# Attention with a gated FFN: the projection block rebuilt, with three and a half FFN chunks beside it instead of two

## What is computed

```
xn  = layernorm(X)
Q, K, V = xn @ Wq.T, xn @ Wk.T, xn @ Wv.T          # 16 heads of 16, rotary positions on Q and K
s   = softmax(causal(Q K.T / 4)) V  @ Wo.T
h   = fwht(xn * SU_ug) / 64                        # Walsh-Hadamard over 256 features
y   = silu(h @ W_gate.T * (..)) * (h @ W_up.T * (..))     # 1024 features
y   = fwht(y * SU_dp) / 64 @ W_down.T * (..)
out = X + s * silu(y)
```

## Time and profile before

| | |
|---|---|
| median of 3 runs | 883.9 us (883.43 to 888.3) |
| the profiled execution | 882.72 us, its span 881.0 us |
| granted TensorE clock, mean | 0.972 |
| TensorE busy | 798.3 us |
| VectorE, ScalarE, GpSimd busy | 574.3, 498.6, 421.1 us |
| block two begins on TensorE | 218.85 us |

### The profile page before, as it was taken

The page is one execution under the profiler, slowest core; times in us unless marked ns, Lnnn a source line. Parts: engine busy times, 40 slices in busy tenths (PEclk is TensorE's granted clock), DMA queues, the critical chain, the costliest instruction groups (busy, mean ns, idle before and its releaser), DMA issues.

```text
span 881.0 us, 14276 instructions
## 1 busy us (share of the span) xinstructions
PE 798.3 (91%) x5136; PEld 482.1 (55%) x5136; DVE 574.3 (65%) x1016; ACT 498.6 (57%) x687; POOL 421.1 (48%) x472
## 2 busy tenths in 40 slices
PE   3767899887989999999999999999999999999976
PEld 2545777766655555555555555555555555555523
DVE  3997455324776777667777677766767666776444
ACT  3434453532455667566775666764676657666560
POOL 3776573563641455225671544543384424745311
PEclk9999999999999999999999999999999999999987
DMA  8445233525502322233344342334433232532131
GB/s 277 155 149 175 69 119 124 174 79 201 124 1 73 89 57 61 86 96 88 94 118 153 111 116 85 85 103 124 125 116 98 89 108 61 167 93 94 57 128 48
DMA packets 61294, 96.21 MB, mean 109 GB/s; under 512 B 10344, under 2 KB 27432, under 8 KB 61224
## 3 DMA queue, kind: packets, MB, share of 16 engines
q1 hardware_dynamic: 59640, 93.47, 34.8%
q10 hardware_dynamic: 1584, 1.84, 0.6%
HBM read 58.06 MB, written 36.95 MB: 108 GB/s over the span
## 4 chain that ended last, share of the span: by engine, by line
PE 60%; DVE 8%; ACT 4%; issue 2%; POOL 1%; ACTq 0%; DVEq 0%; POOLq 0%
PE ps L295 15%; PE ps L1291 13%; PE ps L1275 10%; PE ps L1252 8%; PE ps L305 8%; DVE ps L1526 3%; PE ps L1327 3%; ACT probs L1421 2%; DVE mx L1531 2%; PE ps L1263 2%; ACT x_ffn L1433 1%; DVE ps L1588 1%; DVE y_sb L342 1%; ACT y_sb L330 1%; ACT a_sb L315 0%
## 5 line engine op out<-in xcount | busy, mean ns | idle before, releaser
L1421 ACT ACTIVATE probs<-ps 128x1024 f32<-128x1024 f32 (+1 forms) x320 | 291.7, 940 | 103.6 <-PE ps L1275 102.5
L1531 DVE TENSOR_REDUCE mx<-ps 128x4 f32<-128x512 f32 (+1 forms) x192 | 216.0, 1134 | 110.9 <-PE ps L1252 63.3
L1147 POOL TENSOR_SCALAR_AFFINE_SELECT probs<-probs 128x256 f32<-128x256 f32 (+1 forms) x192 | 92.5, 486 | 271.6 <-ACT probs L1421 271.0
L1526 DVE CUSTOM_DVE_ANT_0 ps<-ps,tri 128x384 f32<-128x384 f32 (+1 forms) x256 | 154.4, 647 | 39.0 <-PE ps L1252 39.0
L1291 PE MATMUL ps<-probs,v_ones 128*32 128x512 f32 (+3 forms) x1536 | 157.7, 498 | 5.5 <-POOL probs L1147 5.0
L1275 PE MATMUL ps<-q_s,k_s 64*128 64x512 f32 (+3 forms) x768 | 147.6, 410 | 8.4 <-ACT probs L1421 4.3
L1275 PEld LDWEIGHTS ps<-q_s,k_s 64*128 64x128 f32 x768 | 67.3, 184 | 151.9 <-issue 79.5
L1252 PE MATMUL ps<-k_s,q_s 48*128 48x512 f32 (+3 forms) x768 | 123.0, 369 | 8.4 <-PEq L386 5.2
L295 PE MATMUL ps<-xh,wug_hi 128*128 128x512 f32 x256 | 110.5, 432 | 16.8 <-DVE a_sb L336 16.4
L350 POOL TENSOR_TENSOR a_sb<-a_sb,u_sb 128x512 f32<-128x512 f32 x64 | 82.2, 1287 | 62.7 <-DVE a_sb L336 34.4
L295 PE MATMUL ps<-xh,wug_lo 128*128 128x512 f32 x256 | 102.8, 402 | 0.0
(11 more groups left out here) (134 smaller groups left out, 1073.9 us busy)
## 6 DMA issues: line engine op xcount, KB each, us to landing
scr_qk<-kinds SPq DMA_DIRECT2D x64, 256.0 KB, 2.3
q_s<-scr_qk SPq DMA_DIRECT2D x64, 128.0 KB, 2.8
...
```

The costliest lines, as they stand in the source:

```text
L1147: pool.affine_select(out=part, in_=part, compare_op=ALU.is_ge, fill=0.0, base=0, pattern=pattern, channel_multiplier=-1).then_inc(cut, 1)
L1421: act.activation(probs[:, n % 2, p, :, 0:w], ps[:, bank:bank + 2, 0:w], ACT.Exp, scale=SCALE).then_inc(exp_ok, 1)
L1526: last = dve.tensor_tensor_reduce(part_of, part_of, sh.tri[:, CH - w:CH], 1.0, LOWEST, ALU.add, ALU.max, mx[:, v % 2, kind, h, i % TPC:i % ...
L1531: last = dve.tensor_reduce(out[:, :, pairs[0]:pairs[0] + n], ps[:, banks[0]:banks[0] + 2, 0:n * w].rearrange('p e (x k) -> p e x k', x=n), ...
```

## The change

Block one:

- `fold_up` is gone. TensorE makes sum and difference by accumulation: four float32 matmuls for a part instead of two, with `had` and a negated copy `minus_had`. All four parts have buffers and are loaded at the start, in the order UG_PARTS. FOLDS puts parts 0 and 1 before k = 0, 2 and 3 into k = 0, and the two of the down weights into k = 1.
- The shift moves from VectorE (`centre`) to GpSimd (inside `rsqrt`), from a small VectorE copy `minus_mean`. The last stage of `fold_down` moves from GpSimd to VectorE, and so does the low part of Q for k = 1 and 2.
- FFN jobs start at k = 1, place 2: chunks 0, 1 and 2 and the first 8 gate and up jobs of chunk 3 run in block one, 80 jobs instead of 48. Gates and ups stand four to a place in places 2 and 3 of odd k and 0 and 1 of the next; downs stand in places 0 and 1 of odd k from 3.
- All 8 PSUM banks are given out by age over the written sequence (`early_banks`), for the projections, the folds and the FFN alike.
- `kinds_low(7, 1)` and `kinds_high(7, 1)` come before the last jobs; gates of an FFN chunk are stored when it is done; FFN_ORDER says which tokens FFN chunk n holds.

Block two: it starts with 112 FFN jobs instead of 144; chunk 3's rest and chunks 4 to 7. The constants are set in z = 0, x for the first 'turn' is loaded first, its normalising is spread over z = 1 to 3, and the split of Wo moves from z = 3 to z = 4. At the end, `divide(6)` moves from round z = 83 to 82, the spreading of the last unit's inverse into round 84, and the high and low parts of chunk 6 behind the rounds.

```diff
-for n, counts in ((0, ((3, (3, 3, 3, 3)), (4, (2, 2, 2, 2)), (5, (2, 2, 0, 0)))),
-                  (1, ((5, (0, 0, 3, 3)), (6, (5, 5, 2, 2)), (7, (1, 1, 1, 1))))):
...
+FFN_ORDER = (4, 0, 1, 2, 3, 5, 6, 7)
...
+NEARLY = 3
...
+for n in range(NEARLY + 1):
     todo = gates_and_ups(n) + downs(n)
-    for k, numbers in counts:
+    for k, numbers in ((2 * n + 1, (0, 0, 4, 4)), (2 * n + 2, (4, 4, 0, 0)), (2 * n + 3, (4, 4))):
+        if k >= NCHUNK:
+            break
...
+UG_PARTS = (2, 0, 3, 1)
+FOLDS = {(-1, 0): (0, 1), (0, 0): (2,), (0, 2): (3,), (1, 1): (4,), (1, 2): (5,)}
+        width = 1 if turn != what or what[0] in ('gate', 'up') else 2
+        sets = [tuple(range(b, b + width)) for b in range(0, 8, width)]
+        banks = min(sets, key=lambda bs: max(held[b][1] for b in bs))
...
-for n in range(2, NCHUNK):
-    todo += gates_and_ups(n)
...
+for n in range(NEARLY, NCHUNK):
+    todo += [j for j in left_over if j[0] != 'down'] if n == NEARLY else gates_and_ups(n)
+    turns = [('turn', n + 1, d) for d in range(DC)] if n + 1 < NCHUNK else []
...
-jobs_at[round_of(NU - 1, 0) + 3].append(('divide', LAST - 1, 0))
+jobs_at[round_of(NU - 1, 0) + 2].append(('divide', LAST - 1, 0))
...
                 pool.tensor_tensor(sh.rstd[:, ORDER[c], :], var_eps[:, :], minus_half[:, :], op=ALU.pow).then_inc(rstd_ok, 1)
+                pool.wait_ge(rstd_ok, c + 1)
+                pool.tensor_tensor(sh.shift_x[:, ORDER[c], :], minus_mean[:, c % 2, :], sh.rstd[:, ORDER[c], :],
+                                   op=ALU.mult).then_inc(centred, 1)
...
+            fold_down(0)
             rsqrt(1)
...
+                    pe.wait_ge(ug_in[i], 16)
+                    for o in range(DC):
+                        pe.matmul(ps[:, bank + o, :], had[:, :], wug[:, i, 0, :], start=True, stop=False)
+                        last = pe.matmul(ps[:, bank + o, :], (minus_had if o else had)[:, :], wug[:, i, 1, :], start=False,
+                                         stop=True)
...
+                if c >= 3 and c % 2:
+                    act.wait_ge(sh.gate_ok, IB * (c - 1) // 2)
+                    act.wait_ge(sh.up_ok, IB * (c - 1) // 2)
...
-            def fold_up(i):
-                dve.wait_ge(ug_in[i % 2], 16 * (i // 2 + 1))
...
+            def fold_down_last():
+                dve.wait_ge(d_fold, 2)
...
+                if z == 0:
+                    constants()
...
             end_high(LAST - 1)
+            high_part(LAST - 1)
             take_heads(NU - 1, 1)
```

More of the change, by code:

```diff
@@ L125 @@
     chain_at[round_of(NU - 1, 0) + later, what] = LAST - 1
-for what, later in (('load', 2), ('recip', 3), ('keep', 4)):
+for what, later in (('load', 2), ('recip', 3), ('keep', 3), ('spread', 4)):
     chain_at[round_of(NU - 1, 0) + later, what] = LAST
@@ L552, in _ @@
                         rsqrt(k + 2)
-                    if place == 2 and k < 3:
+                    if place == 2 and k < 1:
                         queries_low(k)
@@ L593, in features @@
                 bank = pair_at[turn]
[L594 removed]
+                wait_banks(turn)
                 par = c % 2
@@ L651, in fold_weights @@
                 else:
                     pe.wait_ge(d_fold, 3)
-                for o in range(2):
-                    k = 4 * (i - NUG) + 2 * o
-                    rhs = fold[:, i % 2, o, :] if i < NUG else wd[:, 1, k:k + 2, :]
-                    last = pe.matmul(ps[:, bank + o, :], had[:, :], rhs, start=True, stop=True)
+                    for o in range(2):
+                        k = 4 * (i - NUG) + 2 * o
+                        last = pe.matmul(ps[:, bank + o, :], had[:, :], wd[:, 1, k:k + 2, :], start=True, stop=True)
@@ L657, in fold_weights, with folds @@
                 last.then_inc(prod, 1)
+            def folds(k, place):
+                for i in folds_at(k, place):
+                    fold_weights(i)
             pe.wait_ge(ident_ok, 1)
             transposes(0)
+            folds(-1, 0)
             for k in range(NCHUNK):
@@ L667, in _ @@
                     job(j)
+                folds(k, 0)
                 features(k, 1)
@@ L670, in _ @@
                     job(j)
+                folds(k, 1)
                 if k + 1 < NCHUNK:
@@ L674, in _ @@
                     job(j)
+                folds(k, 2)
                 pe.wait_ge(wq_ok, 2)
@@ L678, in _ @@
                     job(j)
-                for i in (2 * k, 2 * k + 1):
-                    if i < NW:
-                        fold_weights(i)
+                folds(k, 3)
         @block.scalar
@@ L860, in jobs @@
                         outer_gate(dve, ps, sh, early_bank[turn_of(j)], *j[1:3])
+                for i in folds_at(k, place):
+                    weights_low(i)
             variances(0)
-            centre(0)
-            weights_rest(0)
-            take_xl(0)
-            variances(1)
-            weights_rest(1)
-            dve.wait_ge(small_in, 32)
+            dve.wait_ge(had_in, 16)
+            dve.tensor_scalar_mul(minus_had[:, :], had[:, :], -1.0).then_inc(had_ok, 1)
+            dve.wait_ge(scales_in, 16)
             dve.tensor_scalar_mul(su_ug_s[:, :], su_ug[:, :], float(D) ** (-0.5)).then_inc(scale_ok, 1)
@@ L974, in second_block @@
         block = ctx.enter_context(nc.Block())
-        pair_round = lambda n, ib: max(job_round['gate', n, ib], job_round['up', n, ib])
+        pair_round = lambda n, ib: max(job_round.get((kind, n, ib), -1) for kind in ('gate', 'up'))
         ups = lambda z: [j for j in jobs_at[z] if j[0] in ('gate', 'up') and z == pair_round(*j[1:])
-                         and (j[0] == 'up' or ('up', *j[1:]) not in jobs_at[z])] if z >= 0 else []
+                         and (j[0] == 'up' or ('up', *j[1:]) not in jobs_at[z])] if z >= 0 else [
+                             j for j in jobs_in(LAST, PLACES - 1) if j[0] == 'up']
         nth_x = lambda n: n - NEARLY - 1
@@ L1487, in _ @@
                     take_heads(u - 1, 1)
-                if at(z, 'high') is not None:
+                if at(z, 'high') is not None and at(z, 'high') < LAST - 1:
                     high_part(at(z, 'high'))
-                if 0 <= z - 1 < NR:
+                if z < NR:
+                    normalise_at(z)
+                if z < NR:
                     for j in ups(z - 1):
@@ L1629, in _ @@
                     invert(at(z, 'recip'))
-                if z >= round_of(NU - 1, 0):
-                    if at(z, 'scale') is not None:
-                        scale_heads(at(z, 'scale'))
-                    if at(z, 'low') is not None:
-                        low_part(at(z, 'low'))
+                if z >= round_of(NU - 1, 0) and at(z, 'scale') is not None:
+                    scale_heads(at(z, 'scale'))
             end_low(LAST - 1)
+            low_part(LAST - 1)
             scale_heads(LAST)
```

301 lines of the change are left out of this document (149 added, 152 removed).

## The result

The changed kernel takes 848.1 us (median of 4 runs, 846.2 to 848.5) where the kernel before, on the same chip, takes 883.7: a ratio of 0.9575 with a 95% interval of 0.9544 to 0.9606, so 4.25% less (by the two medians alone 35.5 us, 4.0%). The profiled execution took 848.0 us with a span of 846.2, 34.8 less than the span before.

A forecast was written before the change was run, and what follows sets the result against it. TensorE was taken to bound attention (z = 6 to 79), while block one had idle time. From 881.0, +9.7 - 2.9 - 29 - 5.6 gave 853.2, with 1.7 around the span 854.9; forecast 856 us, range 842 to 871.

The forecast's parts named there:

- the main case: Whole kernel: both stages, block one and the rounds, go as worked out, 849 to 864 us; chance 0.66.
- z = 0 to 5: Block two's first rounds: matmuls +1.4, wait before the first turn -3.0, less time at 1.2 GHz -1.3; sum -2.9 us.
- Waits in block one: Block one: 8 us of TensorE waits in all, 5 worked out and 3 for the unseen; last job at 225.
- The chain of even k: Block one, k = 2, 4, 6: K, `turn`, `rotate`, `hidden_low`, tanh, up and x's split delay the next X about 1 us each.
- The edge: From block one's last job to block two: 3.5 us, taken between 2.5 and 5.2; block two begins at 228.5, +9.7.
- nothing, or 2 us: z = 1: price if GpSimd's constants, issued in z = 0, delay `hidden` and so the tanh of pair 7.
- The rounds: z = 6 to 79: 31 jobs fewer, 0.82 us saved per job going from two to one, 1.5 from three; -29 us.
- The rival of rounds that don't shrink: z = 6 to 79: thinner rounds run one after another, -18 instead of -29, total 867 us; chance 0.12.
- the one that they shrink whole: z = 6 to 79: TensorE's time comes back whole, -43 instead of -29, total 842 us; chance 0.08.
- The end: Last rounds: fewer jobs in z = 80 -2.3, chunk 6's split behind the last exponentials -3.3; sum -5.6 us.
- The rival on the other side: Block one: its chain holds TensorE, slower than before; block one grows by 36 more, total 891 us; chance 0.07.
- VectorE and GpSimd hinder each other: Block one: some 19 VectorE instructions with both inputs in SBUF take 1.1 us longer; 15 on the path, 870; chance 0.07.

The follow-up runs named there:

- the second profile: The changed kernel run once more, unedited, as the base for two other runs on their chip: 845.9 us, ratio 0.9576 to the kernel before.

## Why the prediction was right, point by point

The forecast was 856, and the median is 848.1: inside the stated 842 to 871, but 1 us under the 849 to 864 of the main case, to which 0.66 was given. 854.9 was predicted for the profiled execution, which took 848.0. Changes of each stage, from the earlier trace rows:

| | predicted | measured |
|---|---|---|
| block two begins | +9.7 | +1.6 (+3.9 in the second profile) |
| z = 0 to 5 | -2.9 | +1.2 (-0.3) |
| z = 6 to 79 | -29 | -32.2 (-33.4) |
| the end | -5.6 | -5.5 (-7.2) |
| span | -27.8 | -34.8 (-36.9) |

The four stages miss by 8.1 us too high, 4.1 too low, 3.2 too high and 0.1 too low. That the sum is only 7 off is in part luck, since the 4.1 stand against the others.

- **Work in block one: right.** The sum of jobs, projections and folds was 194.2; TensorE is busy 194.35. Q(0) began at 21.6 (22.9 taken): the folds at the lower clock cost less than the 2 us.
- **Waits in block one: right in kind and place, too large in size.** The term of 8 us (5 worked out, 3 for what I didn't see) measured 3.4: 0.83 three times and 0.9 once, none over 2. The chain of even k was named, at about 1 us each time, and is the one that shows; the 0.9 stands in k = 1 and is a wait for VectorE's `turn`, where 1 to 2 us were taken for VectorE (its cause is in the last point of this list). The further 3 us for the unseen had nothing behind them.
- **The edge: at the wrong end of its bounds.** I took 3.5 between 2.5 and 5.2, and it is 1.04, under the lower one. The bound counted a tanh, an up and a barrier; the tanh runs under TensorE's last products, and the up's 0.69 and 0.3 of barrier are left. With 48 and with 72 jobs, where nothing stands behind the projections, it is 7.0: the cover by the last eight jobs was the right reason.
- **z = 0 to 5: the step that failed.** The wait of 2.99 before the first turn is gone, as said, and the 1.4 us of matmuls came. But new waits took the gain: in z = 1 TensorE waits 1.71 for a gate's sum on VectorE, after the turn 0.95 and 0.69, in z = 5 0.82, 0.55 and 0.29, and six matmuls after these run at the lower clock. That is 5.0 us of waits where the kernel before had 3.5. In its timeline:

```profile
231.27 2.55 POOL L375 TENSOR_TENSOR a_sb<-a_sb,u_sb 128x512 f32<-128x512 f32 x2
232.60 0.62 ACT L1477 CAST hid_hi<-a_sb 128x512 fp32r<-128x512 f32 x1 [2.33 <-POOL a_sb L375]
...
235.84 0.50 PE L320 MATMUL ps<-xh,wug_hi 128*128 128x512 f32 x1 [1.71 <-DVE a_sb L361]
```

  I had left this open with "nothing, or 2 us", because GpSimd's constants stand ahead of `hidden` in z = 1. It is of that size. The trace leads back to the constants: GpSimd works on block one's last two pairs till 225.5 and on the constants till 231.3, then comes `hidden`, behind it `hidden_high` on ScalarE, the tanh at 234.38, the gate's sum at 235.09 and the product. With 48 and with 72 jobs no pairs are left over at the edge, GpSimd sets the same constants before the first `hidden` is due, and TensorE has no such wait. That the wait goes when the constants do was not shown (the run with them in z = 1 has no profile to read). The second profile of the changed kernel has the same six waits to 0.01 us, but a clock of 1.00 instead of 0.97 and 49.6 us for this stage: 1.5 of the 4 us missed are the clock.
- **The rounds: right, with a term each way.** -32.2 against -29 (place by place 30). The one-job rounds take 6.66, 6.54, 6.99, 6.38 and 6.35 by place in the unit (medians), 32.9 in all against the 33.3 of the earlier trace rows; the two-job rounds 37.8, so that a job is worth 0.98 and not 0.82. With 48 jobs the stage was already 552.0, 4.8 less at one job less, a part that the sum didn't have: four rounds with 'turn' jobs (z = 16, 31, 45, 61) went from 8.34, 8.03, 8.11 and 8.34 to 7.34, 7.13, 6.89 and 7.36, 4.1 in all. The other 30 jobs take off 27.4, 0.91 each, and 1.04 without the 3.8 that the empty round took back. The rival of rounds that don't shrink (867) is out, and so is the one that they shrink whole, at 1.39. The other way, a round with no job was put at 0.5 us under a one-job round: z = 51 with 52 cost 17.2 instead of 13.45 with one job each, and a job put back there gains 1.1 to 3.8, as the clock goes.
- **The end: right.** -5.5 against -5.6, with the mechanism named: the last weighting waits 4.15 us where the split is left in its round and 2.69 where it isn't, and leaving it costs 2 to 4 us. Late next is GpSimd's cut; `low_part`, which the prediction named, holds the first piece by 0.92 in the second profile alone.
- **The rival on the other side** (block one's chain holds TensorE, 891) needed 28 us more of waits and had none. The order of its risk was right all the same: one more pass of GpSimd in seven chunks costs 6.7 us from Q(0) on, and two banks 23.
- **VectorE and GpSimd hinder each other** (870): they do, but not at that price. The mean of VectorE's row with both inputs in SBUF (L848) is 1468 ns, shorter than before (1572), with ten more pairs of GpSimd beside it, and GpSimd's own two are 4% longer (1385 and 1338 against 1330 and 1289). Single instructions show what the means hide. One line's durations, then one long instruction of that line, and two that start together:

```profile
L848 DVE TENSOR_TENSOR kinds<-rot,kinds x15: 1217/1226/2286, 42.9 to 215.6; 128x1024 fp32r<-128x1024 f32 x15
```

```profile
42.86 2.25 DVE L848 TENSOR_TENSOR kinds<-rot,kinds 128x1024 fp32r<-128x1024 f32 x1
...
107.31 1.22 DVE L848 TENSOR_TENSOR kinds<-rot,kinds 128x1024 fp32r<-128x1024 f32 x1
107.32 1.26 POOL L520 TENSOR_TENSOR shift_x<-minus_mean,rstd 128x4 f32<-128x4 f32 x1
```

  The shift takes GpSimd 0.20 to 0.52 us six times, and 1.26 and 1.27 the two times that it starts with such an instruction of VectorE: it ends with that one. At 59.44, during a pass of GpSimd, it is VectorE's that takes 2.29. VectorE's products with the rotary table (L842), which have one input in PSUM, take 1208 to 1226 ns all 16 times. By the timeline this reaches TensorE once. Its wait of 0.9 in k = 1 is for `turn`, which VectorE, with no idle time before it, starts behind the split at 42.86: 2.25 us beside GpSimd's low part of Q (41.63, 2.40) where 1.22 is usual. In the second profile that split takes 3.33 and TensorE waits 1.85. The three waits of 0.83 have another cause: they are the same after k = 2, where a pass of GpSimd was held (two in 3.55), as after k = 4, where none was. So the price on the path is 1 to 2 us in k = 1, and no run here removed it.

The single reason under the table is this. Of the 34.8 us, the larger part came from the new order of the work, block one's waits above all, and not from moving jobs: with the 48 jobs of before the ratio is already 0.9653 and the span 30.8 shorter: block two 24.7 earlier, z = 0 to 5 2.5 longer, z = 6 to 79 4.8 and the end 3.8 shorter. Banks by age are worth some 20 us in this block (two banks again: +24.1 there), accumulation 6.2, the covered edge 6, the end 5. Each was measured in another kernel, so they don't add up to the whole. What I costed as the change's main gain, 32 jobs that the rounds needn't carry, is worth about 4 to 7 us net, and 56 jobs are better by 9 to 12 than 80. My sum came out near because it had these waits in it too, as 16.4 us for the banks and VectorE's 20.4 in k = 1, and because one error stood against the others.
